# Token preparation, value and output weights, and quantisation moved tile by tile into the attention steps of a fused attention and int8 layer

## The reference

```python
def attn(x):                                   # x: (4, 512, 256)
    q, k, v = heads(x @ Wq), heads(x @ Wk), heads(x @ Wv)
    q, k = apply_rope(q, pos), apply_rope(k, pos)
    k, v = repeat(k, 4), repeat(v, 4)          # 8 groups of 4 query heads
    s = where(causal, q @ k.T / sqrt(64), min)
    return (softmax(s) @ v).reshape(b, s, 2048) @ Wo

def ffn(x):
    scale = max(absmax(x), eps) / 127
    q = clip(round(x / scale), -128, 127).astype(int8)
    return (q @ weight.T * scale * w_scale + bias).astype(float16)

x = x + attn(layernorm(x))
x = x + ffn(layernorm(x))
```

## Time and profile before

| what | us |
|---|---|
| median of 3 runs | 881.52 (879.83 to 888.71) |
| the profiled execution | 882.8 |
| its span, first to last instruction | 881.0 |
| start to the first score of step 0 | 74.13 |
| first score of step 0 to first score of step 31 (31 steps) | 726.58 |
| first score of step 31 to the end of its last `add_product` | 29.45 |
| from there to the end | 50.84 |
| busy: TensorE, VectorE, ScalarE, GpSimd | 796.6, 656.1, 631.4, 636.3 |

### The profile page before, as it was taken

One profiled execution on the slowest core, in us unless ns is written; L12 is line 12 of the kernel. 1 busy time (PEld: TensorE's weight loads), 2 busy tenths in 40 slices (PEclk: granted clock), 3 DMA queues, 4 the chain that ended last, 5 costly groups with the idle time before them and its releaser, 6 DMA issues.

```text
span 881.0 us, 23969 instructions
## 1 busy us (share of the span) xinstructions
PE 796.6 (90%) x8488; PEld 669.6 (76%) x8488; DVE 656.1 (74%) x1424; ACT 631.4 (72%) x1762; POOL 636.3 (72%) x521
## 2 busy tenths in 40 slices
PE   2878999999999999999999999999999999999523
PEld 1656888888888888888888888888888888887411
DVE  5793777777777777777777777776777777778897
ACT  1455777777787887777787777777877778777334
POOL 5064788887788888887888888888778888862037
PEclk9996999999999999999999999999999999999755
DMA  9132344444344434443344444444434443331002
GB/s 294 44 71 61 92 99 101 103 103 85 94 101 103 97 95 93 98 100 87 93 97 97 103 103 103 97 89 98 97 87 100 97 100 83 83 84 27 1 25 71
DMA packets 50340, 80.53 MB, mean 91 GB/s; under 512 B 11568, under 2 KB 18480, under 8 KB 50224
## 3 DMA queue, kind: packets, MB, share of 16 engines
q1 hardware_dynamic: 46640, 66.43, 31.9%
q0 software_dynamic: 3584, 12.58, 5.4%
HBM read 18.15 MB, written 2.10 MB: 23 GB/s over the span
## 4 chain that ended last, share of the span: by engine, by line
PE 40%; POOL 22%; issue 9%; DMA 9%; DVE 8%; SPq 6%; ACT 5%; ACTq 0%; POOLq 0%; DVEq 0%
PE x_bank L391 13%; PE t_bank L483 7%; PE s_bank L470 6%; PE s_bank L471 5%; PE o_bank L496 4%; DMA qT<-wv 4%; DMA swp<-raw 4%; POOL raw L317 4%; POOL swp L309 3%; POOL raw L303 3%; POOL wv L325 3%; SPq L219 3%; POOL wg L292 3%; PE s_bank L472 2%; ACT prob L676 2%
## 5 line engine op out<-in xcount | busy, mean ns | idle before, releaser
L676 ACT ACTIVATE prob<-s_bank,neg_max 128x384 f32<-128x384 f32 (+3 forms) x512 | 265.7, 529 | 72.0 <-DVE neg_max L898 71.9
L898 DVE TENSOR_REDUCE neg_max<-s_bank 128x1 f32<-128x384 f32 (+3 forms) x352 | 215.8, 635 | 81.4 <-PE s_bank L472 81.4
L887 DVE SCALAR_TENSOR_TENSOR probT<-t_bank,probT 128x512 f16<-128x512 f32 x320 | 215.9, 683 | 35.9 <-ACT probT L688 32.3
L688 ACT ACTIVATE probT<-t_bank 128x512 f16<-128x512 f32 x320 | 188.1, 598 | 49.5 <-PE t_bank L483 46.7
L483 PE MATMUL t_bank<-ident,prob 128*128 128x128 f32 x1280 | 199.3, 278 | 4.8 <-ACT prob L676 2.6
L470 PE MATMUL s_bank<-kT,qT 128*128 128x384 f32 (+3 forms) x512 | 194.2, 381 | 10.0 <-DMA qT<-wv 9.5
L471 PE MATMUL s_bank<-kT,qT 128*128 128x384 f32 (+3 forms) x512 | 165.7, 324 | 0.0
L391 PE MATMUL x_bank<-xT,wg 128*128 128x512 f32 x576 | 159.1, 412 | 1.6 <-issue 0.8
L309 POOL TENSOR_TENSOR swp<-swp,sin 128x512 f32<-128x512 f32 x96 | 124.4, 1296 | 35.7 <-DMA swp<-raw 35.2
L483 PEld LDWEIGHTS t_bank<-ident,prob 128*128 128x128 f32 x1280 | 136.8, 142 | 14.0 <-issue 7.7
L496 PE MATMUL o_bank<-value,probT 128*128 128x64 f16 x3840 | 138.7, 193 | 0.1
(11 more groups left out here) (94 smaller groups left out, 919.3 us busy)
## 6 DMA issues: line engine op xcount, KB each, us to landing
qT<-wv SPq DMA_DIRECT2D x248, 128.0 KB, 2.3
...
```

The source lines that it names most:

```text
L676: nc.scalar.activation(prob[:, slot:slot + blocks, h, :], s_bank[G % SCORE_BANKS][:, at * n:(at + 1) * n].rearrange("p (k n) -> p k n", n= ...
L688: nc.scalar.activation(turned_half[B % TURNED][HI], t_bank[B % TURN_BANKS][:, :], ACT.Copy, scale=PROB_SCALE).then_inc(probT_hi, 1)
L887: nc.vector.scalar_tensor_tensor(out=turned_half[B % TURNED][LO], in0=t_bank[B % TURN_BANKS][:, :], scalar=PROB_SCALE, in1=turned_half[B % ...
L898: nc.vector.tensor_reduce(neg_max[:, s % 2, u:u + len(heads)], s_bank[G % SCORE_BANKS][:, 0:len(heads) * n].rearrange("p (h n) -> p h n", ...
```

## The change

The opening prepares batch 0 alone: its four tiles are loaded first, each by a DMA of its own, then normalised, turned and multiplied by `wv`. The tables that set the places of step 0's projections (`PROJECT_FIRST` and others) are gone; the opening's order is written out. Statistics of the other 12 tiles are taken at the end of the opening on VectorE.

In the first four steps of each of batches 0 to 2, one tile of the next batch is normalised, turned (into `ot_bank`), split and multiplied by `wv` (into `x_bank`): `next_tile(s)`, 12 steps in all. Chunks 1 to 7 of the output weights are split in steps 1 to 7 (`next_chunk`). In the last four steps of each of batches 1 to 3, one finished tile of the batch before is quantised, multiplied and stored: `done_tile(s)`, again 12 steps; the finished batch's means and inverse roots are made in its third following step (`done_statistics`, s % 8 == 2). The closing keeps the last batch's four tiles. `xT` and `value` hold two batches instead of four; `xn`, `q_real`, `qi` and others have memory of their own; `ot_bank` gets a guard like that of `x_bank` (`take_ot_bank`). The square root on ScalarE becomes a bit trick and three Newton rounds on VectorE, eleven small instructions that each wait for the one before (`normaliser`). The order inside the steps is written anew on all engines; on GpSimd, `rotate_second` and `rotate_first` of the second query tile come earlier, and `keep_low(s + 1, 1)` no longer stands behind the key tile's rotation.

```diff
...
+        def next_tile(s):
+
+            return (s // KV_HEADS + 1) * Q_TILES + s % KV_HEADS if 0 <= s < STEPS - KV_HEADS and s % KV_HEADS < Q_TILES else None
+
+        def next_chunk(s):
+
+            return s + 1 if 0 <= s < WO_CHUNKS - 1 else None
+
+        def done_tile(s):
+
+            return (s // KV_HEADS - 1) * Q_TILES + s % KV_HEADS - Q_TILES \
+                if KV_HEADS <= s < STEPS and s % KV_HEADS >= Q_TILES else None
...
+            for t in range(Q_TILES):
+                sp.dma_start(resid[:, t, :], x_tiles[:, t, :]).then_inc(x_tile_loaded[t], 16)
...
-                sp.dma_start(raw[k][:, :], w_value[k * P:(k + 1) * P, :]).then_inc(wv_loaded, 16)
+                sp.dma_start(wv_raw[k], w_value[k * P:(k + 1) * P, :]).then_inc(wv_loaded, 16)
...
+            sp.dma_start(fw_raw[:, :, :], ffn_weight.rearrange("(t p) k -> p t k", p=P)).then_inc(ffn_loaded, 16)
+            load_wo(0)
+            load_tokens(1)
+            load_wo(1)
+            load_tokens(2)
+            load_tokens(3)
...
-            for s in range(STEPS):
+            rotate_first(1, 1)
+
+            for s in range(STEPS + 1):
+                rotate_second(s + 1, 1)
                 keep_low(s + 1, 0)
-                rotate_first(s + 1, 1)
-                rotate_second(s + 1, 1)
                 rotate_sum(s + 1, 1)
                 rotate_first(s + 1, KEYS)
+                keep_low(s + 1, 1)
                 rotate_second(s + 1, KEYS)
                 rotate_sum(s + 1, KEYS)
-                keep_low(s + 1, 1)
                 keep_low(s + 1, KEYS)
+                rotate_second(s + 2, 0)
+                scale_columns(done_tile(s))
                 split_group_weights(s + 3)
                 load_group_weights(s + 5)
-                rotate_second(s + 2, 0)
+                add_residual(done_tile(s - 1))
                 rotate_first(s + 2, 0)
                 rotate_sum(s + 2, 0)
-
+                rotate_first(s + 2, 1)
...
             def values(t):
...
-                if t >= 2:
+                if t >= Q_TILES:
+                    take_x_bank(v_lo, t + 1)
+                elif t >= 2:
                     pe.wait_ge(v_lo, t - 1)
...
+            ot_bank_free = [(xT_lo, Q_TILES)]
+
+            def take_ot_bank(evacuated, count):
+                pe.wait_ge(*ot_bank_free[0])
+                ot_bank_free[0] = (evacuated, count)
...
+            for t in range(Q_TILES):
+                turn_xn(t)
...
+            project(0, 0)
+            project(0, 1)
+            project(0, KEYS)
+            for t in range(Q_TILES):
                 values(t)
...
             for s in range(STEPS + 1):
                 turn(s, 0)
                 scores(s, 4)
+                turn_output(s - 1, 3)
                 scores(s, 5)
-                project(s + 1, 2)
-                turn_output(s - 1, 3)
+                project(s + 1, KEYS)
                 scores(s, 6)
                 turn(s, 1)
                 attend(s, 0)
                 turn(s, 2)
+                scores(s, 7)
                 out_product(s - 1, 3)
-                scores(s, 7)
                 turn(s, 3)
+                turn_output(s, 0)
...
                 project(s + 2, 0)
-                scores(s, 10)
                 turn(s, 5)
                 attend(s, 1)
                 attend(s, 2)
+                turn_quant(done_tile(s))
                 attend(s, 3)
                 attend(s, 4)
+                ffn_product(done_tile(s))
...
                 attend(s, 5)
                 attend(s, 6)
                 turn(s, 8)
+                turn_xn(next_tile(s))
                 out_product(s, 1)
                 attend(s, 7)
                 turn(s, 9)
                 project(s + 2, 1)
+                scores(s + 1, 0)
                 turn_output(s, 2)
-                scores(s + 1, 0)
                 attend(s, 8)
                 attend(s, 9)
                 scores(s + 1, 1)
                 scores(s + 1, 2)
                 out_product(s, 2)
                 scores(s + 1, 3)
...
+                values(next_tile(s))
...
-            def root(n, tiles):
-                act.wait_ge(ln_step, n * (LN_STEPS + 1) + 1)
-                nc.scalar.activation(root_t[:, tiles], ve[:, tiles], ACT.Sqrt).then_inc(root_done, 1)
...
+                keep_value(next_tile(s - 1))
+                scale_wo(next_chunk(s - 1))
...
+                scale_tile(done_tile(s))
...
+                keep_quant(done_tile(s))
...
+                scale_product(done_tile(s))
...
+                keep_xT(next_tile(s))
...
+            def normaliser(variance, scale, tiles):
+
+                v, y, w = ve[:, tiles], scale[:, tiles], tmp[:, tiles]
+                stepped(nc.vector.tensor_scalar(v, variance[:, tiles, 1], LN_EPS, None, ALU.add))
+                stepped(nc.vector.tensor_scalar(y.bitcast(mybir.dt.int32), v.bitcast(mybir.dt.int32), -0.5, ROOT_BITS,
+                                                ALU.mult, ALU.add))
+                for _ in range(NEWTON):
+                    stepped(nc.vector.scalar_tensor_tensor(out=w, in0=y, scalar=-0.5, in1=y, op0=ALU.mult, op1=ALU.mult))
+                    stepped(nc.vector.tensor_tensor(w, w, v, ALU.mult))
+                    stepped(nc.vector.scalar_tensor_tensor(out=y, in0=w, scalar=1.5, in1=y, op0=ALU.add, op1=ALU.mult))
...
+            aggregate(0, Q_TILES)
+            normaliser(mean_var, rstd, slice(0, Q_TILES))
...
+            wo_low(0)
+            for b in range(1, BATCH):
+                dve.wait_ge(x_loaded[b], 16)
+                for t in range(b * Q_TILES, (b + 1) * Q_TILES):
+                    tile_statistics(t)
+            aggregate(Q_TILES, TOK_TILES)
+            normaliser(mean_var, rstd, slice(Q_TILES, TOK_TILES))
...
+            def done_statistics(s):
+
+                if inside(s) and s % KV_HEADS == 2 and s >= KV_HEADS:
+                    finish_statistics(s // KV_HEADS - 1)
...
+            def normalise_done(f):
...
+                nc.vector.tensor_scalar(done_xn[f % 2], resid[:, token_tile(f), :], done_mean_var[:, f, 0:1],
+                                        done_rstd[:, f:f + 1], ALU.subtract, ALU.mult).then_inc(done_xn_ready, 1)
...
+            def quant_scale(f):
...
+                nc.vector.tensor_reduce(scale, done_xn[f % 2], AX.X, ALU.max,
+                                        apply_absolute_value=True).then_inc(amax_done, 1)
...
             for s in range(STEPS + 1):
-                normalise_output(s - 1, 3)
-                maxima(s, 3)
+                value_low(next_tile(s - 1))
+                wo_low(next_chunk(s - 1))
+                normalise(next_tile(s))
                 maxima(s, 4)
-                maxima(s, 5)
                 keep_probT_low(s, 0)
                 keep_oT_low(s - 1, 3)
+                done_statistics(s)
+                normalise_done(done_tile(s))
+                maxima(s, 5)
                 maxima(s, 6)
                 invert_sums(s, 0)
                 keep_probT_low(s, 1)
+                normalise_output(s, 0)
+                maxima(s, 7)
+                quant_scale(done_tile(s))
+                keep_probT_low(s, 2)
...
                 keep_probT_low(s, 3)
-                early_statistics(s, 2)
+                round_tile(done_tile(s))
+                to_whole(done_tile(s))
+                keep_oT_low(s, 0)
...
+                keep_xT_low(next_tile(s))
...
-            aggregate(0, DONE_TILES, TOK_TILES)
-            normaliser(1, slice(0, DONE_TILES))
...
-            prepare(0)
...
+                last_statistics(s, 2)
+                normalise_output(s, 3)
+                maxima(s + 1, 3)
+                add_bias(done_tile(s))
+
+            finish_statistics(BATCH - 1)
+            first_left = TOK_TILES - Q_TILES
+            for f in range(first_left, first_left + 2):
+                normalise_done(f)
+                quant_scale(f)
+            for f in range(first_left, TOK_TILES + 2):
+                if f < TOK_TILES:
+                    round_tile(f)
+                    to_whole(f)
+                if f + 2 < TOK_TILES:
+                    normalise_done(f + 2)
+                    quant_scale(f + 2)
+                if f >= first_left + 2:
+                    add_bias(f - 2)
```

658 lines of the change are left out of this document (353 added, 305 removed).

## The result

| | us |
|---|---|
| forecast | 855 (828 to 876) |
| before | 881.66, median of 4 (879.83 to 888.71) |
| after | 893.77, median of 4 (892.58 to 895.15) |
| ratio | 1.0123, interval 1.0066 to 1.018 |

The account below looks back on a forecast made before the run. TensorE bounds the steps; opening and closing have room. Opening 41, 31 steps 762.7 (707.4 + 28.9 + 17.6 + 6.0 + 2.8), last step 31.1 and closing 19.5 give span 854.3, hence 855 us (828 to 876).

Parts of the forecast that it names:

- the price of the root chains: Steps 10, 18 and 26: four aggregations and eleven small VectorE instructions in one piece cost 2.0 us each, 6.0 together.
- the third rival: In the steps: VectorE has no room, every added instruction reaches the path, held ones at full length; 960 us span, chance 0.06.
- Opening: Before the steps: preparing only four tiles puts the first score at 41 us (37 to 48) instead of 74.13.
- plain step: Steps 24, 25 and 27, with neither a next nor a finished tile: 22.8 us each.
- Reaches the first maxima at about 42, in time: End of the opening: VectorE finishes statistics and roots of twelve tiles, 8 to 9 us, without delaying step 0's first maxima.
- Steps with value products: Twelve steps with a next tile: TensorE work 1.61 us plus 0.8 of waits, taken as 2.4 each, 28.9 together.
- Finished-tile steps: Eleven of the 31 steps: TensorE work 0.39 us plus 1.2 of stall, 1.6 each, 17.6 together; such steps at 24.4.
- Chunks: Seven chunks of output weights split in the steps: 0.88 us of VectorE each, 0.4 on the path, 2.8 together.
- Last step and closing: After the 31 steps: last step 31.1 us with one finished tile more, closing with four tiles 19.5 instead of 50.84.
- The base: The 31 steps without added work: better order brings each from 23.44 to 22.82 us, 707.4 together, upper end 726.6.
- the second rival: In the steps: the new order gains nothing in the steps' own time, 19.2 us more, 874 in all; chance 0.14.
- It decides from 64.5 us of growth: In the steps: VectorE shortage makes the kernel slower once they grow 64.5 us, 2.7 on each of 24 steps.

Follow-up runs that it names:

- the two runs that took 16 and 22 us back: Two edits of the changed kernel: GpSimd waits in steps 10, 18 and 26 until the eleven root instructions are done, 877.48 us; those instructions spread singly over steps, 871.45 us.
- The dealt chain: Changed kernel with a finished batch's eleven root instructions placed one by one, three places a step, in steps s % 8 = 0 to 3: 871.45 us.

## Why the prediction was wrong

The step that failed is the price of the root chains: "four aggregations and eleven small ones, 2.9 of VectorE in one piece ahead of maxima: 2.0 each, 6.0", and the same chain in the opening at "eleven dependent small instructions at 0.21 from start to start (2.3)". I took the 0.21 from the closing of before, where GpSimd has nothing to do, and set it where GpSimd is busy. Measured were 4.3 to 7.2 us a chain where GpSimd was busy, 2.1 and 2.2 in the two chains where it was idle, and with TensorE's clock 6.0, 6.1 and 8.0 a step (against the neighbours 9 and 11, 17 and 19, 25), 20 in place of 6. That is the largest term that failed, but not the only one: without these 14.2 us the kernel would stand at 879.6, still outside the range. The prediction had the mechanism in hand: the earlier trace rows show the hold, and the third rival applied it to normalisations, roundings and bias. It was left off the small instructions, in the forecast and in the rival (which booked 2.9 for the roots too), because their own work is short. What counts is the GpSimd instruction that they meet.

The Trainium skill (SBUF - State Buffer, section SBUF: two separate sides) puts it as an exclusive lock on a shared port pair that the loser waits out, also for an instruction with two SBUF inputs beside a GpSimd instruction that reads SBUF. The chain's rows agree: 0.16 alone, 1.2 behind a GpSimd instruction of 1.3. The 58 cycles that the prediction took from the Trainium skill (VectorE: DVE Perf Modes, section on the TRN2 errata) are the figure of a table; below it the section puts the measured fixed term at about 150 cycles, for a copy, which makes an estimate of 0.16 us for four elements. The rows of 0.16 to 0.17 agree with that, so the Trainium skill does not speak for shorter chains.

Of the 39.0 us between the forecast's span of 854.3 and 893.3:

- Opening, +4.0. The first chain took 7.24 instead of 2.3; the first normalisation began at 14.27, where two were to be done by 9.4. That the hold was the cause of all 4 is not shown, since taking it off the chain put it on the next instructions.
- Step 0, +5.8 over a plain step. "Reaches the first maxima at about 42, in time" was wrong by 5.7: 47.73. How much of the 5.8 is due to that is not shown, since step 0 took 25.1 to 29.0 with the same opening.
- Steps 10, 18 and 26, +14.2, as above; shown by the two runs that took 16 and 22 us back, 15.6 of it in these three steps and 19.9 in the twelve steps around them.
- The other steps, +12.9. Steps with value products: 9, 11, 17 and 19 took 25.70 on average, forecast 25.2; 12 and 20, which have a finished tile too, took 25.78, forecast 26.8. TensorE's own part was 1.9 (24.77 in step 19 to 22.89 in step 25), forecast 1.61. Finished-tile steps: 13 to 15 and 21 to 23 took 25.06, forecast 24.4; VectorE's seven pieces for a tile came to 4.1 in the mean (3.35 for the four big ones in the groups above, 0.73 for the other three), forecast 3.2. Chunks: steps 1 to 3 took 1.4 more than those with value products alone, forecast 0.4; VectorE's part of a chunk (L933) took 1.27 in the mean, forecast 0.88, and stood ahead of the maxima. Plain steps: 8, 16, 24, 25 and 27 took 5.3 more together than five times 22.82 (8 and 16 hold a next tile's normalisation and turn).
- Last step and closing, +2.2, with the chain at 2.14, forecast 2.3, GpSimd being idle there.

The base was too low as well. 31 x 22.82 = 707.4 lies below the 712.53 for which TensorE was busy in these steps before, so that waits were worth at most 14 of the 19.2 that the prediction booked as gained; 22.82 was the time of the fastest full steps there. Step 25 came to 22.91, but the mean of 24, 25 and 27 is 23.47, which the prediction had named as the second rival's sign, and the first score still waits for queries (view of waits in the 31 steps: us in total, times, longest):

```profile
PE s_bank L531 <- DMA qT<-query_parts: 5.9, 9, 1.2
```

Before, that wait was 9.1 in 11 steps: 3.2 of it went.

Opening and closing were right but for the sizes above. The third rival had the right side, and the hold in it, at 960 a far too high price: the earlier trace rows's hold for every added instruction at full length on the path. The dealt chain shows why that is too much: held links that stand singly where VectorE waits cost little (step 26 with three of them took 23.36, beside 22.91 for step 25). "It decides from 64.5 us of growth" was met with 69.0, but not by its terms: its sign, finished-tile steps above 26, did not come (25.06), and it too had the roots at 2.9. A version of the change without long pieces takes 856.7, the time that I had forecast for this one; the agreement is partly chance, since its start differs too.
